# Two fused attention layers on one core: the first two key tiles of a unit are multiplied by halves of the tokens, x's high part before its low part, and the query product takes high parts before low parts

## The chip, the cores and the metric

One NeuronCore of a Trainium2 chip runs the whole program. The metric is the device time of one execution in microseconds (us); lower is better. Engines are called as in the profile: PE multiplies matrices, PEld is its load of the stationary operand, DVE, ACT and POOL are the vector, scalar and GpSimd engines, and SP issues most of the DMAs.

## The reference, cut to what matters

Two layers of the same form run one after the other over x, 8 batches of 512 tokens by 512 features, in float32. With `heads` = 8 in layer 0 and 16 in layer 1:

```python
xn  = layernorm(x) * ln_w + ln_b
q   = softmax_over_features_of_a_head(xn @ Wq + bq)
k   = softmax_over_tokens(masked(xn @ Wk + bk))
v   = masked(xn @ Wv + bv)
att = einsum("bnhd,bnhl->bhdl", k, v)          # layer 1: the same, other letters
y   = einsum("bnhd,bhdl->bnhl", q, att)
h   = silu(layernorm(y) * (1 + scale) + shift)  # scale, shift: a small product of emb
x   = x + h @ W_out + b_out
```

## The kernel before, in words

A **unit** is one batch of one layer; there are 16 (`UNITS`), u = 0 to 15, in the order of the batches, layer 0 first. Every float32 operand of a large product is split into a float16 high part and a float16 low part, and a product is the sum of three: high by high, high by low, low by high (`split_pairs`, and `product` at line 534, where nearly all matmuls are recorded).

PE does the units one after the other. In unit u (`step`) it makes, in this order:
- **K**: `project_keys(u)`, four tiles of 128 key features by 512 tokens. A tile is 4 chunks of the features by 3 products, 12 matmuls of 512 columns, with the weights as the stationary operand and x transposed (`xt_hi`, `xt_lo`, in the tile `xt_parts`) as the moving one. In the rows these read `ring<-sb_xt_parts,sb_w_hi` and `...,sb_w_lo`.
- **V** and **Q**: `project_tokens`, again 48 matmuls each, with x as the stationary operand (`ring<-sb_w_hi,sb_xt_parts`).
- **A**: `attention(u)`, 96 small matmuls (line 658; in unit 0 line 690).
- **O**: `output(u - 1)`, 48 matmuls of the unit before, from `ht_hi` and `ht_lo` (tile `ht_parts`).
- **Y**: `attend(u)`, 96 matmuls of 64 columns (line 709): the queries transposed (`qt_hi`, `qt_lo`, which lie in the tile `k_or_qt`) by the attention matrix.

The last unit (`last_unit`) has Q before V and splits O; unit 0 (`first_unit`) starts with `first_keys`, which is not changed.

The other engines follow: DVE takes each tile of the ring out of PSUM (`masked_keys`, `values`, `queries`, `residual`), does the statistics of Y (`attended_all`: `attended` line 1130, `y_statistics`, `centre` line 1147, which frees a bank pair of Y) and a part of each softmax. Its order in a unit is written out: `keys_beside_h`, `values`, `queries`, `mask_attention`, `query_sums`, the four `residual`s (line 1120, x_new), then `attended_all`. ACT has the exponents, the tanh and the high parts, POOL the low parts.

**The transposes** are DMAs from SBUF to SBUF, issued by SP in an order written out by hand in its `step(u)`: keys (`turn_k`), h (`turn_h`), the first two token tiles of the next unit's x (`turn_x(u, 0)`), queries (`turn_q`), the last two token tiles of x (`turn_x(u, 1)`), each the high part and then the low part:

```python
turn_k(u)
turn_h(u)
...
load_rows(u)
if u < LAST:
    turn_x(u, 0)
turn_q(u)
if u < LAST:
    turn_x(u, 1)
```

A completed transpose raises `xt_hi_ready` or `xt_lo_ready` by 16, so both stand at 32 * u when all of the x of unit u is turned and at 32 * u - 16 when its first half is. `step` and `last_unit` of the kernel before wait for both at 32 * u ahead of K, and `attend` for `qt_hi_ready` and `qt_lo_ready` ahead of its first matmul.

**PSUM**: the ring has six banks. `previous_users` works out from the order of all tiles who must have left a bank, and `take_bank` waits for it. K tiles 0 to 3 use banks 0 to 3. Banks 0 and 1 were O tiles 2 and 3 of the unit before (freed by `residual`), banks 2 and 3 hold the first pair of Y (freed by `centre`).

Of the kernel before, what the change touches and what calls it, by code (L numbers as in the profile page):

```python
# [5 lines left out]
P = 128  # L6
LAYERS = 2
B, S, D, E = 8, 512, 512, 1024
T = S // P
C = D // P  # L10
# [39 lines left out]
def layer_of(u):  # L50
    return u // B
# [55 lines left out]
def build(nc, x_d, emb_d, mask0_d, mask1_d, w_d, bias_d, wemb_d, cols_d, ident_d, blocks_d, out_d):  # L107
    with ExitStack() as ctx:
# [105 lines left out]
        def tile(buffer, a, b):  # L214
            return buffer[:, (4 * a + b) * P:(4 * a + b + 1) * P]
# [29 lines left out]
        def att_count(u):  # L245

            return C + u + (C - 1 if u == LAST else 0)
# [271 lines left out]
        def _(pe):  # L519
# [44 lines left out]
            def project_keys(u, tiles=range(C), between=lambda i: None):  # L564
                hi, lo = w_hi[layer_of(u)][K_], w_lo[layer_of(u)][K_]
                for i in tiles:
# [3 lines left out]
                                             lambda c: xt_hi[:, :, c, :], lambda c: xt_lo[:, :, c, :])).then_inc(done["K"], 1)  # L570
                    between(i)

            def project_tokens(name, unit, m, a_hi, a_lo, tiles=range(T), between=lambda i: None):
                hi, lo = w_hi[layer_of(unit)][m], w_lo[layer_of(unit)][m]
                for i in tiles:
                    out = take_bank(name, i, unit)
                    product(out, split_pairs(lambda c: a_hi[:, i, c, :], lambda c: a_lo[:, i, c, :],
                                             lambda c: hi[:, c, :], lambda c: lo[:, c, :])).then_inc(done[name], 1)
                    between(i)
# [110 lines left out]
                                last = nc.tensor.matmul(att_ps[:, c, :], lhs, rhs, start=(c == t == n == 0), stop=(c == C - 1 and t == T - 1 and n == 2))  # L690
                last.then_inc(att_summed, 1)

            def attend(u, between=lambda t: None):
                pe.wait_ge(qt_hi_ready, 16 * (u + 1))
                pe.wait_ge(qt_lo_ready, 16 * (u + 1))
                if u not in Q_FIRST:
                    pe.wait_ge(att_lo_ready, att_count(u))
                for t in range(T):
                    if t % 2 == 0:
                        take_bank("Y", t, u)  # L700
                    for c in range(C):
                        if u in Q_FIRST and t == 0:
                            pe.wait_ge(att_lo_ready, (att_count(u - 1) if u else 0) + c + 1)
                        hi, lo = tile(qt_hi, t, c), tile(qt_lo, t, c)
                        pairs = ((hi, att_hi), (hi, att_lo), (lo, att_hi))
                        for n, (lhs, rhs) in enumerate(pairs):
                            for j in range(2):
                                g = slice(j * HALF, j * HALF + HALF)
                                last = nc.tensor.matmul(y_at(t)[:, j, c * HALF:c * HALF + HALF], lhs[g, :], rhs[g, c, g], start=(n == 0), stop=(n == 2))  # L709
                    last.then_inc(done["Y"], 1)  # L710
                    between(t)

            def first_unit():
                def with_k(i):
# [32 lines left out]
            def step(u):  # L747
                shifted = PREPARED[1][u - PREP] if PREP <= u < PREP + 3 else None

                def with_k(i):  # L750
                    if u == 3 and i == 3:
                        turn_table(1)

                def with_q(i):
                    if u == 2 and i < 2:
                        film_product(1, i)
                    if shifted is not None and i == 0:
                        pe.wait_ge(h_ready, 4 * u)
                        shift_parts(1, shifted)
                    elif shifted is not None and i == 2:  # L760
                        shift_sums(1, shifted)

                def with_o(i):
                    if u == 2 and i == 0:
                        turn_film(1)
                    elif u == 2 and i == 3:
                        bound_film(1)
                    if PREP <= u < PREP + 4 and i == 3:
                        sum_w(1, PREPARED[1][u - PREP])

                pe.wait_ge(xt_hi_ready, 32 * u)
                pe.wait_ge(xt_lo_ready, 32 * u)
                if u == B:
                    pe.wait_ge(w_ready[1], 1)
                project_keys(u, between=with_k)
                if u == B:
                    pe.wait_ge(w_ready[1], 2)
                project_tokens("V", u, V_, xt_hi, xt_lo)
                if u == B:
                    pe.wait_ge(w_ready[1], 3)  # L780
                project_tokens("Q", u, Q_, xt_hi, xt_lo, between=with_q)
                if shifted is not None:
                    pe.wait_ge(shift_folded, folded(1, shifted))
                pe.wait_ge(h_ready, 4 * u)
                attention(u)
                if u == 1:
                    pe.wait_ge(o0_ready, 1)
                if u == B + 1:
                    pe.wait_ge(w_ready[1], 4)
                pe.wait_ge(ht_hi_ready, 16 * u)  # L790
                pe.wait_ge(ht_lo_ready, 16 * u)
                output(u - 1, between=with_o)
                attend(u)

            def last_unit(u):
                pe.wait_ge(xt_hi_ready, 32 * u)
                pe.wait_ge(xt_lo_ready, 32 * u)
                project_keys(u)
                project_tokens("Q", u, Q_, xt_hi, xt_lo)
                project_tokens("V", u, V_, xt_hi, xt_lo)  # L800
                pe.wait_ge(ht_hi_ready, 16 * u)
# [1050 lines left out]
```

## Time and profile before

| | us |
|---|---|
| median of 3 executions | 802.58 (800.82 to 805.05) |
| span of the profiled execution, first to last instruction | 799.5 |
| PE busy | 761.5 (95%) |
| DVE busy | 697.7 (87%) |
| ACT busy | 517.5 (65%) |
| POOL busy | 438.5 (55%) |
| DMA engines, share of 16 engines' time in the queue of SP | 70.8% |

The profiled execution's own time is its span and the start and end around it; it is one of the kind of the three above, and 802.58 - 799.5 = 3.1 us is what lies around the span at the median. The profile is read by the idle time that stands in front of a group or an instruction and by what released it. A completed DMA transpose is not shown as a releaser: a wait for it reads "issue". A matmul's end is modelled, so PE seems busy for a further 0.2 to 0.4 us after its last start; start to start is the sure reading.

### The profile page before, as it was taken

Reading aid. Unit: us, or ns where it says so; the run is one execution under the profiler, and the core shown is the slowest. Engines: PE = TensorE matmul, PEld = TensorE weight load, DVE = VectorE, ACT = ScalarE, POOL = GpSimd, SP = SyncE. Lnnn points to the kernel's source line nnn. Section 1 sums busy time; section 2 is a strip of 40 time slices with the busy share of each in tenths; the row PEclk is TensorE's granted clock in tenths of the full one; section 3 lists DMA queues with packets and bytes.
Section 4 is the critical chain, followed back from the end, with each engine's and each line's share of the span. In section 5 each row is a group of like instructions: output and inputs, shape, how many; then the busy total and the mean of one; then the engine's idle time right before and its main releaser. Section 6 shows DMA issues by size and latency. Waiting matters only on the chain.

```text
span 799.5 us, 16864 instructions
## 1 busy us (share of the span) xinstructions
PE 761.5 (95%) x6359; PEld 370.6 (46%) x6359; DVE 697.7 (87%) x1427; ACT 517.5 (65%) x1011; POOL 438.5 (55%) x433
## 2 busy tenths in 40 slices
PE   5997999999999999998999999999999999999986
PEld 2445444454544445444444544444454544444442
DVE  7898978798998999999988898898888889888885
ACT  5896766666667686885856685665767575560633
POOL 2465573663737767486672755447364545546323
PEclk9997999999999999999999999999999999999999
DMA  9976895856939769595794939487684939477462
GB/s 327 297 142 183 253 184 176 158 139 162 182 128 158 198 137 201 134 200 148 137 220 87 204 93 180 151 159 198 99 198 113 190 123 185 112 139 153 80 132 80
DMA packets 291249, 130.73 MB, mean 164 GB/s; under 512 B 261440, under 2 KB 261824, under 8 KB 291168
## 3 DMA queue, kind: packets, MB, share of 16 engines
q1 hardware_dynamic: 288432, 125.27, 70.8%
q10 hardware_dynamic: 2736, 4.39, 1.5%
q8 instruction: 50, 0.82, 0.4%
q14 instruction: 31, 0.25, 0.1%
HBM read 47.74 MB, written 16.88 MB: 81 GB/s over the span
## 4 chain that ended last, share of the span: by engine, by line
PE 85%; DVE 9%; issue 3%; ACT 2%; DMA 0%; POOL 0%; SPq 0%; DVEq 0%; ACTq 0%; POOLq 0%
PE ring L534 75%; PE ring L709 3%; PE att_ps L658 3%; DVE sb_k_or_qt L1042 1%; DVE sb_row_peak L881 1%; ACT sb_k_or_qt L1440 1%; DVE sb_q_sum L1101 1%; PE ring L834 0%; PE att_ps L595 0%; PE film_ps L595 0%; DVE sb_q_max L1075 0%; DVE ring L1072 0%; DVE sb_ht_parts L1158 0%; PE film_ps L604 0%; DMA sb_x<-in_x 0%
## 5 line engine op out<-in xcount | busy, mean ns | idle before, releaser
L534 PE MATMUL ring<-sb_w_hi,sb_xt_parts 128*128 128x512 f16 x1024 | 309.0, 379 | 0.0
L534 PE MATMUL ring<-sb_w_lo,sb_xt_parts 128*128 128x512 f16 x512 | 194.0, 379 | 0.0
L534 PE MATMUL ring<-sb_w_hi,sb_ht_parts 128*128 128x512 f16 x512 | 155.8, 379 | 4.0 <-ACT sb_ht_parts L1610 1.4
L534 PEld LDWEIGHTS ring<-sb_w_hi,sb_xt_parts 128*128 128x128 f16 x1024 | 100.4, 98 | 126.0 <-issue 6.6
L534 PE MATMUL ring<-sb_xt_parts,sb_w_hi 128*128 128x512 f16 x496 | 148.6, 381 | 9.7 <-issue 9.1
L1698 POOL TENSOR_TENSOR sb_htok<-sb_ht_parts,sb_htok 128x512 f16<-128x512 f32 x60 | 75.0, 1272 | 137.8 <-ACT sb_htok L1473 137.8
L1714 POOL TENSOR_TENSOR sb_tanh<-sb_v_or_q,sb_kq_hi 128x512 f16<-128x512 f32 x64 | 74.1, 1159 | 87.7 <-ACT sb_kq_hi L1504 87.1
L534 PE MATMUL ring<-sb_w_lo,sb_ht_parts 128*128 128x512 f16 x256 | 97.0, 379 | 0.0
L534 PE MATMUL ring<-sb_xt_parts,sb_w_lo 128*128 128x512 f16 x248 | 94.5, 381 | 0.0
L1497 ACT ACTIVATE sb_v_or_q<-ring,sb_ln_one 128x512 f32<-128x512 f32 x64 | 43.9, 686 | 61.0 <-DVE ring L1077 60.9
L1689 POOL TENSOR_TENSOR sb_x<-sb_x,sb_bias_o 128x512 f32<-128x512 f32 x64 | 79.3, 1274 | 5.9 <-DVE sb_w_lo L958 5.9
L534 PEld LDWEIGHTS ring<-sb_w_hi,sb_ht_parts 128*128 128x128 f16 x512 | 50.1, 98 | 63.4 <-ACT sb_ht_parts L1610 4.1
L534 PEld LDWEIGHTS ring<-sb_xt_parts,sb_w_hi 128*128 128x128 f16 x496 | 47.5, 98 | 67.2 <-issue 12.3
L534 PEld LDWEIGHTS ring<-sb_w_lo,sb_xt_parts 128*128 128x128 f16 x512 | 50.1, 98 | 59.4 <-issue 0.7
L1709 POOL TENSOR_TENSOR sb_tok<-sb_v_or_q,sb_tok 128x512 f16<-128x512 f32 x56 | 66.4, 1199 | 17.1 <-ACT sb_tok L1436 17.1
L1417 ACT ACTIVATE sb_v_parts<-sb_x,sb_x_minus 128x512 f16<-128x512 f32 x52 | 36.9, 710 | 58.4 <-POOL sb_x_minus L1670 58.4
L1120 DVE SCALAR_TENSOR_TENSOR sb_x<-ring,sb_down_o,sb_x 128x512 f32<-128x512 f32 x60 | 43.2, 748 | 28.3 <-PE ring L534 26.0
L1042 DVE SCALAR_TENSOR_TENSOR sb_k_or_qt<-sb_k_or_qt,sb_k_recip,sb_kq_hi 128x512 f16<-128x512 f32 x64 | 61.5, 961 | 5.1
L1440 ACT ACTIVATE sb_k_or_qt<-sb_k_or_qt,sb_k_shift 128x512 f32<-128x512 f32 x64 | 45.4, 710 | 20.3 <-DVE sb_k_shift L1029 20.3
L1432 ACT ACTIVATE sb_v_or_q<-sb_x,sb_x_add,sb_x_rstd 128x512 f32<-128x512 f32 x56 | 43.9, 808 | 22.2 <-POOL sb_x_add L1677 22.2
L1464 ACT ACTIVATE att_ps<-sb_ht_parts,sb_scale_down 128x512 f32<-128x512 f32 x30 | 20.6, 687 | 57.6 <-DVE sb_ht_parts L1153 57.5
L1072 DVE SCALAR_TENSOR_TENSOR ring<-ring,sb_scale_down,sb_bias_q 128x512 f32<-128x512 f32 x64 | 48.0, 750 | 9.1 <-PE ring L534 9.0
(232 smaller groups left out, 1401.0 us busy)
## 6 DMA issues: line engine op xcount, KB each, us to landing
out<-sb_x SPq DMA_DIRECT2D x14, 1024.0 KB, 4.9
sb_rows_now<-film_rows SPq DMA_DIRECT2D x16, 512.0 KB, 4.5
sb_x<-out SPq DMA_DIRECT2D x8, 1024.0 KB, 5.2
sb_x<-in_x SPq DMA_DIRECT2D x7, 1024.0 KB, 5.4
sb_mask_add<-mask_terms SPq DMA_DIRECT2D x15, 256.0 KB, 5.5
sb_w_hi<-in_L_cond_W_emb SPq DMA_DIRECT2D x1, 1536.0 KB, 14.1
sb_w_lo<-in_L_cond_W_emb SPq DMA_DIRECT2D x1, 1536.0 KB, 14.4
sb_w_hi<-in_L_cond_film_emb_W ACTq DMA_DIRECT2D x1, 1536.0 KB, 11.9
```

The lines of the kernel that those rows point to most:

```text
L534: last = nc.tensor.matmul(out, lhs, rhs, start=(n == 0), stop=(n == len(pairs) - 1))
L1042: nc.vector.scalar_tensor_tensor(out=k_lo[:, i * S:i * S + S], in0=k_or_qt[:, i, :], scalar=k_recip[:, i:i + 1], in1=kq_hi[:, i * S:i * S ...
L1072: nc.vector.scalar_tensor_tensor(out=here, in0=here, scalar=scale_down[:, layer, Q_:Q_ + 1], in1=bias_q[layer][:], op0=ALU.mult, op1=ALU.a ...
L1120: nc.vector.scalar_tensor_tensor(out=xt(unit, t), in0=bank("O", t, unit), scalar=down_o[:, layer:layer + 1], in1=xt(unit, t), op0=ALU.mult ...
L1417: nc.scalar.activation(unused(unit)[:, t, :], xt(unit, t), ACT.Square, bias=x_minus[:, t:t + 1], accum_out=x_square[:, t:t + 1]).then_inc( ...
L1432: nc.scalar.activation(xh_of(unit)[:, t, :], xt(unit, t), ACT.Identity, bias=x_add[:, t:t + 1], scale=x_rstd[:, t:t + 1]).then_inc(xh_read ...
L1440: nc.scalar.activation(k_or_qt[:, i, :], k_or_qt[:, i, :], ACT.Exp, bias=k_shift[:, i:i + 1], accum_out=k_sum[:, i:i + 1]).then_inc(k_exp, 1)
L1497: nc.scalar.activation(q[:, t, :], bank("Q", t, u), ACT.Exp, bias=ln_one[:]).then_inc(q_exp, 1)
L1689: nc.gpsimd.tensor_tensor(xt(u, t), xt(u, t), bias_o[layer][:], ALU.add).then_inc(x_biased, 1)
L1698: nc.gpsimd.tensor_tensor(hp_lo[:, t, :], y_of(unit)[:, t, :], hp_hi[:, t, :], ALU.subtract).then_inc(h_lo_ready, 1)
L1709: nc.gpsimd.tensor_tensor(xp_lo[:, t, :], xh_of(unit)[:, t, :], xp_hi[:, t, :], ALU.subtract).then_inc(xp_lo_ready, 1)
L1714: nc.gpsimd.tensor_tensor(q_lo[:, t * D:t * D + D], q[:, t, :], kq_hi[:, t * D:t * D + D], ALU.subtract).then_inc(q_lo_ready, 1)
```

## The change

A new `keys_by_halves(u)` makes key tiles 0 and 1 of the units 1 to 15. It takes both banks at the start, then waits only for the first half of the tokens (both parts) and makes all three products of both tiles for tokens 0 to 255; then it waits for the second half of x's high part and makes the two products that use it; then for the second half of the low part and makes the last one. That is 24 + 16 + 8 = 48 matmuls of 256 columns in place of 24 of 512. Tile 0 and tile 1 are both finished in the last eight. Tiles 2 and 3 follow by `project_keys(u, (2, 3))` as before. `attend` takes its token tiles in two pairs: for a pair the products with the high queries come first (32 matmuls), then, for the first pair, the wait for `qt_lo_ready`, then those with the low queries (16 matmuls). The number of its matmuls is the same. SP, DVE, ACT and POOL have the same instructions in the same order.

```diff
+            def keys_by_halves(u):
+
+                hi, lo = w_hi[layer_of(u)][K_], w_lo[layer_of(u)][K_]
+                outs = [take_bank("K", i, u).rearrange("p (t m) -> p t m", t=T) for i in range(2)]
+                pe.wait_ge(xt_hi_ready, 32 * u - 16)
+                pe.wait_ge(xt_lo_ready, 32 * u - 16)
+                for i in range(2):
+                    f = slice(i * P, i * P + P)
+                    for c in range(C):
+                        for n, (w, xs) in enumerate(((hi, xt_hi), (hi, xt_lo), (lo, xt_hi))):
+                            nc.tensor.matmul(outs[i][:, 0:2, :], w[:, c, f], xs[:, 0:2, c, :], start=(c == n == 0), stop=False)
+                pe.wait_ge(xt_hi_ready, 32 * u)
+                for i in range(2):
+                    f = slice(i * P, i * P + P)
+                    for c in range(C):
+                        for w in (hi, lo):
+                            nc.tensor.matmul(outs[i][:, 2:4, :], w[:, c, f], xt_hi[:, 2:4, c, :], start=False, stop=False)
+                pe.wait_ge(xt_lo_ready, 32 * u)
+                for i in range(2):
+                    f = slice(i * P, i * P + P)
+                    for c in range(C):
+                        last = nc.tensor.matmul(outs[i][:, 2:4, :], hi[:, c, f], xt_lo[:, 2:4, c, :], start=False, stop=(c == C - 1))
+                    last.then_inc(done["K"], 1)
+
...
-            def attend(u, between=lambda t: None):
+            def attend(u):
                 pe.wait_ge(qt_hi_ready, 16 * (u + 1))
-                pe.wait_ge(qt_lo_ready, 16 * (u + 1))
                 if u not in Q_FIRST:
                     pe.wait_ge(att_lo_ready, att_count(u))
-                for t in range(T):
-                    if t % 2 == 0:
-                        take_bank("Y", t, u)
-                    for c in range(C):
-                        if u in Q_FIRST and t == 0:
-                            pe.wait_ge(att_lo_ready, (att_count(u - 1) if u else 0) + c + 1)
-                        hi, lo = tile(qt_hi, t, c), tile(qt_lo, t, c)
-                        pairs = ((hi, att_hi), (hi, att_lo), (lo, att_hi))
-                        for n, (lhs, rhs) in enumerate(pairs):
+                for pair in ((0, 1), (2, 3)):
+                    take_bank("Y", pair[0], u)
+                    for t in pair:
+                        for c in range(C):
+                            if u in Q_FIRST and t == 0:
+                                pe.wait_ge(att_lo_ready, (att_count(u - 1) if u else 0) + c + 1)
+                            for n, part in enumerate((att_hi, att_lo)):
+                                for j in range(2):
+                                    g = slice(j * HALF, j * HALF + HALF)
+                                    nc.tensor.matmul(y_at(t)[:, j, c * HALF:c * HALF + HALF], tile(qt_hi, t, c)[g, :], part[g, c, g],
+                                                     start=(t % 2 == c == n == 0), stop=False)
+                    if pair[0] == 0:
+                        pe.wait_ge(qt_lo_ready, 16 * (u + 1))
+                    for t in pair:
+                        for c in range(C):
                             for j in range(2):
                                 g = slice(j * HALF, j * HALF + HALF)
-                                last = nc.tensor.matmul(y_at(t)[:, j, c * HALF:c * HALF + HALF], lhs[g, :], rhs[g, c, g], start=(n == 0), stop=(n == 2))
-                    last.then_inc(done["Y"], 1)
-                    between(t)
+                                last = nc.tensor.matmul(y_at(t)[:, j, c * HALF:c * HALF + HALF], tile(qt_lo, t, c)[g, :], att_hi[g, c, g],
+                                                        start=False, stop=(t == pair[1] and c == C - 1))
+                        last.then_inc(done["Y"], 1)
...
-                pe.wait_ge(xt_hi_ready, 32 * u)
-                pe.wait_ge(xt_lo_ready, 32 * u)
                 if u == B:
                     pe.wait_ge(w_ready[1], 1)
-                project_keys(u, between=with_k)
+                keys_by_halves(u)
+                project_keys(u, (2, 3), between=with_k)
...
             def last_unit(u):
-                pe.wait_ge(xt_hi_ready, 32 * u)
-                pe.wait_ge(xt_lo_ready, 32 * u)
-                project_keys(u)
+                keys_by_halves(u)
+                project_keys(u, (2, 3))
```

## Rows read from the trace of the kernel before

**Rows 1.** The page: busy time and share of each engine, and the granted clock.
```profile
PE 761.5 (95%) x6359; PEld 370.6 (46%) x6359; DVE 697.7 (87%) x1427; ACT 517.5 (65%) x1011; POOL 438.5 (55%) x433
PEclk9997999999999999999999999999999999999999
```

**Rows 2.** Chain that ended last, 540 to 640 us: start, us, what.
```profile
548.42 0.31 issue
548.73 31.24 PE ring L534 x144
...
592.07 1.51 PE ring L709 x96
593.58 0.49 issue
```

**Rows 3.** Groups of the page: busy, mean ns of one, idle before them, releaser.
```profile
L534 PE MATMUL ring<-sb_xt_parts,sb_w_hi 128*128 128x512 f16 x496 | 148.6, 381 | 9.7 <-issue 9.1
```

**Rows 4.** Timeline of PE where K starts: start us, us, what, idle before it.
```profile
122.36 0.59 PE L534 MATMUL ring<-sb_xt_parts,sb_w_hi 128*128 128x512 f16 x2 [1.48 <-issue]
...
365.12 0.59 PE L534 MATMUL ring<-sb_xt_parts,sb_w_hi 128*128 128x512 f16 x2 [2.19 <-issue]
411.36 0.59 PE L534 MATMUL ring<-sb_xt_parts,sb_w_hi 128*128 128x512 f16 x2 [0.85 <-issue]
...
503.56 0.59 PE L534 MATMUL ring<-sb_xt_parts,sb_w_hi 128*128 128x512 f16 x2 [1.01 <-issue]
...
594.07 0.59 PE L534 MATMUL ring<-sb_xt_parts,sb_w_hi 128*128 128x512 f16 x2 [0.49 <-issue]
594.50 0.38 PE L534 MATMUL ring<-sb_xt_parts,sb_w_lo 128*128 128x512 f16 x1
...
730.98 0.59 PE L534 MATMUL ring<-sb_xt_parts,sb_w_hi 128*128 128x512 f16 x2 [1.20 <-issue]
```

**Rows 5.** Timeline of SP's queue, transposes of queries and x, late in unit 11.
```profile
586.55 2.54 SPq L410 DMA_TRANSPOSE sb_k_or_qt<-sb_tanh  x1
589.21 2.89 SPq L410 DMA_TRANSPOSE sb_xt_parts<-sb_tok  x2
```

**Rows 6.** DMA issues: count, median us to landing.
```profile
sb_xt_parts<-sb_tok SPq DMA_TRANSPOSE x60, 3.8
```

**Rows 7.** Timeline of PE: the seam from Y to K where nothing is waited for.
```profile
221.39 0.20 PE L709 MATMUL ring<-sb_att_hi,sb_k_or_qt 64*128 64x64 f16 x2
221.51 0.61 PE L534 MATMUL ring<-sb_xt_parts,sb_w_hi 128*128 128x512 f16 x2
```

**Rows 8.** Timeline of PE where Y or O starts late, four places.
```profile
350.78 0.38 PE L534 MATMUL ring<-sb_w_hi,sb_ht_parts 128*128 128x512 f16 x1 [0.52 <-issue]
408.93 0.20 PE L709 MATMUL ring<-sb_att_hi,sb_k_or_qt 64*128 64x64 f16 x2 [0.47 <-issue]
500.97 0.21 PE L709 MATMUL ring<-sb_att_hi,sb_k_or_qt 64*128 64x64 f16 x2 [0.60 <-issue]
771.49 0.21 PE L709 MATMUL ring<-sb_att_hi,sb_k_or_qt 64*128 64x64 f16 x2 [1.67 <-issue]
```

**Rows 9.** Timeline of PE, 128-column matmuls of unit 0, from 62.80 us.
```profile
62.80 1.17 PE L690 MATMUL att_ps<-sb_v_parts,sb_kt_or_y 128*128 128x128 f16 x18
```

**Rows 10.** Timeline of PEld at the start of K in unit 12.
```profile
594.04 0.13 PEld L534 LDWEIGHTS ring<-sb_xt_parts,sb_w_hi 128*128 128x128 f16 x2 [0.59 <-issue]
```

**Rows 11.** Timeline of DVE around the starts of K in units 7 and 8.
```profile
361.41 0.75 DVE L1120 SCALAR_TENSOR_TENSOR sb_x<-ring,sb_down_o,sb_x 128x512 f32<-128x512 f32 x1 [0.32 <-PE ring L534]
...
365.41 1.30 DVE L1130 TENSOR_TENSOR ring<-ring,sb_q_recip 128x512 f32<-128x512 f32 x2
...
368.30 1.40 DVE L1147 SCALAR_TENSOR_TENSOR sb_ht_parts<-ring,sb_y_mean_var,sb_rows_now 128x512 f32<-128x512 f32 x2
...
408.57 0.75 DVE L1120 SCALAR_TENSOR_TENSOR sb_x<-ring,sb_down_o,sb_x 128x512 f32<-128x512 f32 x1 [1.84 <-PE ring L534]
409.85 1.30 DVE L1130 TENSOR_TENSOR ring<-ring,sb_q_recip 128x512 f32<-128x512 f32 x2 [0.53 <-PE ring L709]
...
418.75 0.74 DVE L1021 CUSTOM_DVE_ANT_0 sb_k_or_qt<-ring,sb_mask_add,sb_scale_down 128x512 f32<-128x512 f32 x1
```

## The prediction

> **What bounds the kernel now.** I read the page first. PE is busy 95% of the span and runs at full clock but for one slice; DVE follows with 87% [rows 1]. Then the chain of waits, in order of time. One unit is 45.2 us there (548.42 to 593.58), and all of it is PE but a piece called "issue" between Y and K: 0.31 us ahead of unit 11, 0.49 ahead of unit 12 [rows 2]. So there is little to win except these pieces. The groups add them up: the first matmuls of K have 9.7 us of idle time ahead of them, 9.1 of it "issue" [rows 3]. The timeline shows them one by one, nine of over 0.2 us, the longest 1.48 in unit 2 and 2.19 in unit 7 [rows 4].
>
> What is waited for is a transpose, which the profile does not name as a releaser. In unit 11, SP issues the low queries' transpose at 586.55 and the two of x's second half at 589.21 to 592.10; the low one goes out near 590.7, and with the median of 3.8 us to landing it arrives at about 594.5 [rows 5, 6]. K starts at 594.07 [rows 4]. The first half of x was turned ahead of the queries. So the wait is for the last quarter of x, the low part of the second half, and the high part is there some 1.4 us sooner.
>
> **The change part by part.**
>
> *The waits ahead of K.* The stalls sum to 9.1 us [rows 3]. Idle time is counted from a modelled end 0.2 us after the last start of Y, and with no wait K starts 0.12 us after that start [rows 7], so each of the nine is 0.08 longer: 9.1 + 9 * 0.08 = 9.8 us. In the new order the last quarter is needed only after 40 matmuls of 256 columns, 40 * 0.109 = 4.4 us after K starts (pace below), the high one after 24, 2.6 us. The longest stall is 2.27 us, so each is covered with 2 us in hand. Removed: **9.8 us**.
>
> *The matmuls.* 24 of 512 columns become 48 of 256. Two of 512 start 0.43 us apart, 215 ns each [rows 4]; 18 of 128 columns with a full 128 by 128 load each take 1.17 - 0.22 = 0.95 us from first to last start, 56 ns each [rows 9]. A line through the two is 0.415 ns a column and 2.8 ns a matmul, so one of 256 takes 109 ns. Price: 24 * 2.8 = 0.07 us a unit, 15 units: **1.0 us**. Bounds: nothing (if half the columns took half the time), and 24 * 8.5 = 0.2 us a unit, 3 us in all, if each 256 columns ran at the pace of two 128s. The line lies between them, and I take it. The loads are 24 more too. That a load hides behind 128 columns is in rows 9: the pace there, 56 ns, is the columns' own. The Trainium skill (TensorE: Matmul & The Clock Gate, section "Back-to-back issue gap") speaks against that: a stream of loads and matmuls of 128 columns takes about 81 ns each. By it a matmul of 256 columns would take an estimated 134 ns and the change would cost 18 us, not 1. The trace does not agree, with 56 ns where the page says 81.
>
> *Tile 0 done later.* It was done 2.6 us after K's start and is now done after 44 matmuls, 4.8 us. DVE waits for it, but DVE is on the statistics of Y until 418.75, when it turns to key tile 0, 7.4 us after that K's start [rows 11]. Cost nothing; if DVE were over 2.6 us faster there it would be up to 2.2 us a unit.
>
> *Bank 1 taken early.* Tile 1's bank is now wanted at K's start, not 2.6 us later. It is freed by the last residual, which ends at 408.57 + 0.75 = 409.3, while Y is still running and 2 us ahead of that K [rows 11]. Nothing.
>
> *Y with the high queries first.* 32 matmuls before the wait for the low ones. 96 take 1.39 us (592.07 to 593.58, less the seam of 0.12) [rows 2, 7], so 32 are 0.46 us of cover. Three late starts of Y are 0.47, 0.60 and 1.67 us [rows 8]. Each gives up to 0.46, together **1.4**; the lower end is 1.0, if the low queries come later against PE than now. The first pair is finished no later than before, so DVE loses nothing.
>
> *What is late next.* DVE's order from Y to the next queries has hardly a wait for PE in it, and behind it hang ACT's and POOL's parts and the transposes of h and queries. That path starts at the end of O (residual) or the first pair of Y and takes about as long as PE's round, and it does not get shorter when K starts sooner. Three places:
> - Unit 7, with the 2.27 us stall. DVE was late there: it finished the last residual at 362.2, then did scales until 365.41, and the two centres that free banks 2 and 3 end at 368.30 + 1.40 = 369.7 [rows 11]. K would now start at 362.85, want bank 2 at + 5.2 = 368.1, and wait 1.6 us for it. Add 0.3 at O, whose h comes down the same path: 1.9 of the 2.27 given back.
> - O in units 6, 8 and 10. In unit 6 O already waited 0.52 us for h [rows 8] with almost no stall ahead of K. In units 8 and 10 the stalls ahead of K were 0.93 and 1.09 (idle and 0.08) [rows 4]; I take half as given back, 1.0, and 0.1 for unit 6. Ends: none and all 2.0.
> - Unit 15, where Y waits 1.67 us for its queries [rows 8], which do not come from PE's progress alone: 0.5 of its 1.28 us [rows 4] back.
>
> In all **3.5 us** given back; the ends are 1 us (no h wait, a centre that comes sooner) and 7 (every later unit bound by DVE's path).
>
> **Sum:** 9.8 + 1.4 - 1.0 - 3.5 = 6.7 us off the profiled span of 799.5: 792.8, and with the 3.1 us around it **795.9 us** against the median of 802.58 (0.8% less).
>
> **The rivals.**
> 1. *The other engines' path sets the round* (DVE's order, then ACT, POOL and the transposes of h and queries). For it: DVE is 87% busy [rows 1], Y and O each have waits for transposes [rows 8], and PE is at most 1 us a unit behind that path. Against it: DVE stands idle for 1.84 us each unit waiting for O's last tile [rows 11], so the path restarts with PE, not by itself. If it held in units 7 to 15, the gain left would be that of unit 2 (1.5), Y's 1.4 and about 0.8 from the rest, less 1.0 for the matmuls: 802.6 - 2.7 = 799.9 us.
> 2. *Slower: the loads are no longer hidden.* Place: the 48 matmuls of each `keys_by_halves`. Where nothing covers a load the matmul starts 31 ns after it, 594.04 to 594.07 [rows 4, 10]. If each of the 720 new matmuls lost that, 22 us: 795.9 + 22.3 = 818 us. It decides against the change from 6.7 us / 720 = 9 ns a matmul. Against it: 56 ns for 128 columns [rows 9]. The page named above gives 25 ns of such a loss, an estimated 814 us.
> 3. *The stall is not the transpose.* If "issue" were PE's own start of a new shape, it would stay, and the change would cost its 1.0 us: 803.6. Against it: a seam with no stall at all [rows 7] and lengths from 0.31 to 2.19 [rows 2, 4].
> 4. *Nothing is given back.* 9.8 + 1.4 - 1.0 = 10.2 us off: 792.4.
>
> **How the numbers follow.** A change under 0.5% (4.0 us) is what a measurement of this kernel can hardly tell from none; three runs spread over 4.2 us. Forecast (3 to 9 us off, faster by over 0.5% in most of it): 0.74. Rival 1: 0.16. Rival 2: 0.04. Rival 3: 0.03. Rival 4: 0.03. Faster by over 0.5% (below 798.6): nearly all of the forecast and rival 4, 0.76. Within: rivals 1 and 3 and the weak end of the forecast, 0.20. Slower: 0.04. The range runs from just below rival 4's end, 792.0, to 799.6, just short of rival 1, and so leaves out some 2 in 10.
>
> **What would show it.** Right: "issue" ahead of K's matmuls goes from 9.1 us to under 1; the 256-column matmuls start 109 ns apart; in unit 7 PE waits 1 to 2 us in the middle of K for DVE line 1147; a new or longer wait stands ahead of O in units 8 and 10; Y starts with less idle time. Wrong: starts 120 ns apart or more; DVE newly waiting for key tile 0; waits ahead of O and inside Y that sum to 6 us or more; or K's stall still there in its last eight split matmuls.

## The result, and the profile after

The changed kernel takes **791.65 us** (median of 4 runs, 790.94 to 793.91) against 802.03 us for the kernel before, run beside it: ratio 0.9881 [0.9864, 0.9898], faster by 1.2%. On the median the prediction was made against, 802.58, that ratio gives 793.0 us, inside the predicted 792.0 to 799.6. The raw median lies 0.35 us under the low end. The profiled execution spans 789.9 us (own time 791.66), 9.6 us less than before. The sum had said 6.7.

The page of the changed kernel, answering to [rows 1] and to the group of [rows 3], and below it, from the list of groups, the group that K now starts with:

```profile
PE 761.1 (96%) x6719; PEld 405.4 (51%) x6719; DVE 696.8 (88%) x1427; ACT 517.4 (65%) x1011; POOL 439.4 (56%) x433
...
PEclk9998999999999999999999999999999999999999
...
L534 PE MATMUL ring<-sb_xt_parts,sb_w_hi 128*128 128x512 f16 x256 | 76.2, 379 | 1.8 <-DVE sb_ht_parts L1174 1.8
...
L583 PE MATMUL ring<-sb_xt_parts,sb_w_hi 128*128 128x256 f16 x240 | 41.5, 278 | 0.0
```

PE does 360 matmuls more in the same busy time (761.1 us, 761.5 before), so what went is idle time. The 9.1 us of "issue" in that group is gone, the 256-column group at K's start has no idle time ahead of it, and 1.8 us of a wait for DVE are new.

The changed kernel's chain of waits, 540 to 600 us (start, us, what), against [rows 2]:

```profile
541.93 0.47 PE ring L730 x32
542.39 0.23 PE ring L738 x16
542.63 2.73 PE ring L583 x24
545.36 1.75 PE ring L589 x16
547.10 0.87 PE ring L594 x8
547.98 25.90 PE ring L534 x120
...
587.48 2.73 PE ring L583 x24
```

The unit is now 44.85 us (542.63 to 587.48), and no "issue" stands between Y (lines 730, 738) and K (583, 589, 594). Before it was 45.2.

The changed kernel's PE, waits by the line that waited (us in total, times, longest), without those that stand in the first and last units:

```profile
PE ring L534 <- DVE sb_ht_parts L1174: 1.8, 2, 1.5
...
PE ring L534 <- issue: 1.2, 3, 0.6
...
PE ring L738 <- DMA sb_k_or_qt<-sb_tanh: 0.7, 2, 0.4
```

Three lines answer to three steps of the prediction: a wait in the middle of K, what is left of "issue" (ahead of O in units 6 and 7 and in the last unit, none ahead of K), and the low queries, now waited for separately.

The changed kernel's timeline of PE, the four places that matter (start us, us, what, idle before it):

```profile
367.99 0.60 PE L534 MATMUL ring<-sb_xt_parts,sb_w_hi 128*128 128x512 f16 x2 [1.49 <-DVE sb_ht_parts L1174]
...
587.42 0.39 PE L583 MATMUL ring<-sb_xt_parts,sb_w_hi 128*128 128x256 f16 x2
587.65 0.27 PE L583 MATMUL ring<-sb_xt_parts,sb_w_lo 128*128 128x256 f16 x1
587.75 0.38 PE L583 MATMUL ring<-sb_xt_parts,sb_w_hi 128*128 128x256 f16 x2
...
721.39 0.41 PE L738 MATMUL ring<-sb_att_hi,sb_k_or_qt 64*128 64x64 f16 x16 [0.27 <-DMA sb_k_or_qt<-sb_tanh]
...
762.33 0.41 PE L738 MATMUL ring<-sb_att_hi,sb_k_or_qt 64*128 64x64 f16 x16 [0.43 <-DMA sb_k_or_qt<-sb_tanh]
```

Three matmuls of 256 columns take 587.75 - 587.42 = 0.33 us from start to start, 0.11 each. The wait at 367.99, in K of unit 7, is for DVE's centre, as foretold.

**Where the 9.6 us came from**, start to start, units 1 to 15 summed, after minus before:

```
last Y start -> first K start    -10.07   (before: 10.1 over 0.12 each; after: 0)
K, first to last start            +2.51   (unit 7: +1.74; the other fourteen: +0.77)
K's end -> O's start              +0.30   (unit 7: 0.29; units 6, 8, 10: 0.05, 0.00, 0.04)
O                                 -0.05
O's end -> last Y start           -2.11   (unit 7 -0.54, 9 -0.67, 15 -1.13, 10 +0.08, 14 +0.15)
ahead of unit 1's K               -0.20
```

### The profile page after: what moved, and what is told of

Same layout as the page of the kernel before. It is cut to its first block, busy times and chain, and to the rows that moved or that the text cites. A ratio compares the mean times of both kernels' runs of the same rounds, so it can differ in the third digit from the quotient of the medians.

```text
span 789.9 us, 17598 instructions
## 1 busy us (share of the span) xinstructions
PE 761.1 (96%) x6719; PEld 405.4 (51%) x6719; DVE 696.8 (88%) x1427; ACT 517.4 (65%) x1011; POOL 439.4 (56%) x433
## 4 chain that ended last, share of the span: by engine, by line
PE 80%; DVE 12%; ACT 3%; issue 2%; DMA 2%; SPq 1%; POOL 0%; DVEq 0%; ACTq 0%; POOLq 0%
PE ring L534 62%; PE ring L583 5%; PE ring L589 3%; PE att_ps L682 3%; PE ring L730 2%; PE ring L594 1%; DVE sb_k_or_qt L1069 1%; DMA sb_k_or_qt<-sb_tanh 1%; ACT sb_k_or_qt L1467 1%; PE ring L738 1%; DVE sb_row_peak L908 1%; DVE sb_q_max L1102 1%; DVE ring L1099 1%; DVE ring L1104 1%; DVE sb_q_sum L1128 1%
## 5 line engine op out<-in xcount | busy, mean ns | idle before, releaser
L534 PE MATMUL ring<-sb_xt_parts,sb_w_hi 128*128 128x512 f16 x256 | 76.2, 379 | 1.8 <-DVE sb_ht_parts L1174 1.8
L534 PE MATMUL ring<-sb_xt_parts,sb_w_lo 128*128 128x512 f16 x128 | 48.5, 379 | 0.0
L1180 DVE SCALAR_TENSOR_TENSOR sb_ht_parts<-sb_ht_parts,sb_y_rstd,sb_rows_now 128x512 f32<-128x512 f32 x60 | 47.1, 805 | 0.0
```

The lines of the kernel that those rows point to most:

```text
L534: last = nc.tensor.matmul(out, lhs, rhs, start=(n == 0), stop=(n == len(pairs) - 1))
L1180: nc.vector.scalar_tensor_tensor(out=y_of(unit)[:, t, :], in0=y_of(unit)[:, t, :], scalar=y_rstd[:, t:t + 1], in1=rows_now[:, 1, :], op0=A ...
```

## The experiments

Each kernel was timed in three rounds beside the kernel before on its chip; a ratio is to that. The "changed kernel" is the one of the diff.

### Each half alone

**The keys' part alone**: the changed kernel with the old `attend`.

```
-            def attend(u):                          # the changed one
+            def attend(u, between=lambda t: None):  # the one before
```

> The key tiles by halves alone, the query product as before. Theory A (the stall ahead of K was the wait for x's last quarter, and the other engines' path is not the bound): 'issue' ahead of K under 1 us, the gain 8 to 9.5 us of the whole change's 10; Y keeps late starts of up to 0.5 us in the units where its low queries land last. Theory B (the other engines' path sets the round, and the gain needs the later wait in Y as well): under 6 us, with more idle time ahead of Y than before.

Measured: 794.28 us, ratio 0.9912 [0.9893, 0.9931], 7.1 us off. At the median this is less than theory A's band and more than theory B's (the interval gives 5.5 to 8.6 us), so neither can be said to have had it right. All K stalls are gone (-10.07), K is 2.94 longer, and Y starts late. Its PE timeline and wait list:

```profile
497.43 0.20 PE L733 MATMUL ring<-sb_att_hi,sb_k_or_qt 64*128 64x64 f16 x2 [0.87 <-issue]
...
764.62 0.20 PE L733 MATMUL ring<-sb_att_hi,sb_k_or_qt 64*128 64x64 f16 x2 [1.94 <-issue]
```

```profile
PE ring L733 <- issue: 3.5, 4, 1.9
```

The 0.87 and 1.94 us ahead of the first matmul of Y were 0.60 and 1.67 before [rows 8]: with K early, the queries come a little later against PE. So Y's order seems to be worth more on top of the first part than the 1.4 of the prediction: 794.28 less 791.65 or, in the later run below, 792.46 is 2.6 or 1.8 us. The intervals of the ratios overlap slightly, so the times alone don't prove it; stage by stage the two profiles differ by 2.8 us from O's end to Y's.

**Y's part alone**: the kernel before with the new `attend`.

```
-            def attend(u, between=lambda t: None):  # the one before
+            def attend(u):                          # the changed one
```

> The query product's new order alone, K as before. Theory A: Y's late starts shrink, but K still waits for x's last quarter, which lands a fixed time behind the queries, so what Y gains is waited for ahead of K: the time is the same within 1.5 us, and the idle time ahead of K grows. Theory B: 1.4 us or more faster, since the first pair of Y restarts DVE sooner.

Measured: 800.24 us, 0.9988 [0.9977, 1.0], no difference beyond the measurement. Theory A had the time right but not the way there: in the profile Y gave 1.27, and K's stalls did not grow but shrank by 1.64. But K of unit 7 is 1.7 us longer, because the clock fell. In the windows view of this kernel (columns: window, its length, busy time of PE, PEld, DVE, ACT and POOL, granted clock, DMA share, GB/s):

```profile
361.50:364.90 3.40, 1.66 (x99) 1.52 (x97) 2.98 (x10) 0.00 (x0) 3.40 (x4) 1.00 1.19 185
364.90:368.50 3.60, 3.44 (x9) 1.23 (x10) 3.38 (x10) 2.71 (x7) 0.85 (x2) 0.53 0.51 196
368.50:371.90 3.40, 3.40 (x17) 1.54 (x16) 3.37 (x9) 1.69 (x5) 2.08 (x4) 1.00 0.72 264
```

After a stall of 1.97 us the granted clock averages 0.53 over the next 3.6 us (the level of 1.2 GHz nearly throughout) where the kernel before, after a stall of 2.27, kept 1.00. The columns took the time and PE was "busy" meanwhile, so no list of waits shows this loss.

### Is it the transpose, and are the loads hidden?

**The split with none of its use**: both waits for x stand at K's start, 256 columns, old `attend`.

```
             def keys_by_halves(u):
...
-                pe.wait_ge(xt_hi_ready, 32 * u - 16)
-                pe.wait_ge(xt_lo_ready, 32 * u - 16)
+                pe.wait_ge(xt_hi_ready, 32 * u)
+                pe.wait_ge(xt_lo_ready, 32 * u)
```

(and the two later waits are gone)

> The 256-column matmuls alone: both key tiles are made by halves, but all four waits for x stand at the start, and the query product is as before. My price of 2.8 ns a matmul: 1.0 us slower than before, starts 109 ns apart. Rival (loads no longer hidden, 31 ns each): 22 us slower. Half-size matmuls at no price: the same.

Measured: 803.82 us, 1.0027 [1.0016, 1.0038], 2.2 us slower (1.3 to 3.0), more than my 1.0. Rival 2's 22 us are excluded: K goes from 10.14 to 10.20 us, 0.06 a unit, 0.8 us in all. In the profile the largest other piece is again the clock, in unit 10. The other executions agree: their mean granted clock is 0.992 (ten), against 0.995 for the kernel before (twenty). The PE timeline and the wait list of this kernel:

```profile
502.62 0.58 PE L583 MATMUL ring<-sb_xt_parts,sb_w_hi 128*128 128x256 f16 x2 [2.45 <-DMA sb_xt_parts<-sb_tok]
503.01 0.42 PE L583 MATMUL ring<-sb_xt_parts,sb_w_lo 128*128 128x256 f16 x1
503.22 0.63 PE L583 MATMUL ring<-sb_xt_parts,sb_w_hi 128*128 128x256 f16 x2
...
503.86 0.63 PE L583 MATMUL ring<-sb_xt_parts,sb_w_hi 128*128 128x256 f16 x2
```

```profile
PE ring L583 <- DMA sb_xt_parts<-sb_tok: 9.9, 9, 2.5
```

Three matmuls take 0.64 us there (503.22 to 503.86), twice as long as at full clock, and that K is 11.78 us long, 1.6 more. And the stall that was called "issue" is now named: a wait for x's transpose, 9 times, 9.9 us. A DMA that is waited for can appear under either name.

**SP's order**: the kernel before, with x's second half turned ahead of the queries.

```
+                if u < LAST:
+                    turn_x(u, 1)
                 turn_q(u)
                 if u < LAST:
-                    turn_x(u, 1)
                     sp.wait_ge(x_new, 4 * u)
```

> The kernel before with one change in SP's order: the transposes of x's second half are issued ahead of the queries' ones instead of behind them; PE's program is untouched. Theory A: SP is idle between the last Q tile on PE and the last high query, about 4 us, and the two issues take 2.9, so the queries' transposes are hardly later, x is there when Y ends, and the stalls ahead of K vanish without 256-column matmuls: 8 to 11 us faster. Theory C (the transposes share the DMA engines, and an earlier one for x makes the one for the queries late): the idle time moves from K to Y, and the gain is under 4 us.

Measured: 805.64 us, 1.0059 [1.0039, 1.0079], slower. The queue in unit 11 (timeline of SP), and the wait list of PE:

```profile
579.95 7.33 SPq L410 DMA_TRANSPOSE sb_xt_parts<-sb_tok  x4
587.47 1.36 SPq L410 DMA_TRANSPOSE sb_k_or_qt<-sb_kq_hi  x1
588.95 3.49 SPq L410 DMA_TRANSPOSE sb_k_or_qt<-sb_tanh  x1
```

```profile
PE ring L710 <- issue: 15.0, 12, 2.3
```

Theory C had it: the idle time moved from K to Y, for a loss. K's stalls are all gone (-10.07), which shows that they are the transposes of x's second half, last in SP's queue, and rival 3 falls. But the low queries' transpose is issued later: at 588.95, 38.5 us after the start of its unit's K, where it was 37.8 us [rows 2, 5]. Y starts late, by 0.65 us more in this unit and by 12.7 us more in sum. One transfer is last in this queue; the change under study makes that one harmless instead of moving it.

### Is the split needed?

**High part first, 512 columns**: the changed kernel, where K's first two tiles are taken whole, 16 high matmuls, then the wait, then 8 low ones (the loops shortened to words).

```
-                pe.wait_ge(xt_hi_ready, 32 * u - 16)
...
+                pe.wait_ge(xt_hi_ready, 32 * u)
+                for i in range(2): ...   w_hi, w_lo x xt_hi[:, :, c, :]
+                pe.wait_ge(xt_lo_ready, 32 * u)
+                for i in range(2): ...   w_hi x xt_lo[:, :, c, :]
```

> The changed kernel with keys_by_halves replaced: both tiles keep 512 columns, K waits at its start for all of x's high part, makes 16 matmuls with it, and only then waits for the low part (3.5 us later). Query product as in the changed kernel. If only the last quarter of x was late, and the split into 256 columns is paid for: 1 us faster than the changed kernel (about 12 less than the kernel before), less what K now waits for the high part, which landed 0.1 to 0.7 us ahead of K's start in most units. If the first half's early start matters too: 1 to 3 us slower than the changed kernel.

Measured: 793.38 us, 0.9918 [0.9903, 0.9933]. Three short stalls come back ahead of K (0.26, 0.30 and 0.34 us, units 2, 8 and 10), and its profile has a fall of the clock in the last unit, worth 1.5 us. So most of the gain, 6.6 us of some 9, needs no halves at all, only the high part ahead of the low one. But I had expected it to be 1 us faster than the changed kernel, and it is 2 to 3 us slower: its interval lies just above the 0.9881 [0.9864, 0.9898] of the result and overlaps the later 0.989 [0.9873, 0.9908]. That is the size foretold for the case that the first half's early start matters; the profile, with 0.9 us of stalls ahead of K, shows a part of it only.

**One tile by halves**: tile 0 split, tile 1 whole and high part first (the edit in words).

```
-                for i in range(2):     # both tiles [:, 0:2, :], then [:, 2:4, :]
+                tile 0: xt[:, 0:2], wait high, xt_hi[:, 2:4]; tile 1: xt_hi whole;
+                wait low; tile 0: xt_lo[:, 2:4]; tile 1: xt_lo whole
```

> The changed kernel with only key tile 0 by halves; tile 1 keeps 512 columns, high part first: 12 matmuls of 256 columns need the first half alone (1.3 us), then come 8 of 256 and 8 of 512 with the high part (2.6 us), so the last quarter of x is wanted 3.9 us after K's start. It landed 1.1 to 2.7 us after it in the changed kernel and the high part at most 0.3 us after it, so nothing stalls, and K is 24 * 1.4 ns = 0.03 us shorter: 0.5 us faster than the changed kernel, or the same as far as three rounds tell. If the high part is wanted too early: PE waits at line 587 or so in several units, slower than the changed one.

Measured: 795.21 us, 0.9921 [0.9899, 0.9943]. No stall ahead of K, and the extra matmuls cost about half, as expected. But it is not 0.5 us faster: at the median it is 2.8 us slower than the changed kernel run beside it (792.46; the intervals overlap). Half a us of that lies outside the span (2.3 us around it, 1.8 in the others), and in its profile the low queries were later in units 9 and 15. Its timeline of PE:

```profile
498.09 0.41 PE L739 MATMUL ring<-sb_att_hi,sb_k_or_qt 64*128 64x64 f16 x16 [1.38 <-DMA sb_k_or_qt<-sb_tanh]
...
764.43 0.41 PE L739 MATMUL ring<-sb_att_hi,sb_k_or_qt 64*128 64x64 f16 x16 [1.08 <-DMA sb_k_or_qt<-sb_tanh]
```

In unit 9 the low transpose landed 4.2 us after the high one, not the usual 2.3. Whether this comes from the edit or from the run stays open.

### The 1.5 us in unit 7

**The scales later**: the changed kernel; in unit 6, whose scales DVE does from 360.3 to 363.6 in the changed kernel's timeline, they are moved behind `attended_all`.

```
-                if prepares is not None:
+                if prepares is not None and prepares != O_:
                     find_scale(1, prepares)
-                if prepares == O_:
-                    output_scale(1)
-                    v_scales(1)
                 attended_all(u)
+                if prepares == O_:
+                    find_scale(1, prepares)
+                    output_scale(1)
+                    v_scales(1)
```

> The changed kernel; in unit 6 DVE's scale work for the last weight of layer 1 (13 small instructions, 3.2 us) stands behind the statistics of Y instead of ahead of them. My step: the 1.49 us that PE waits in K of unit 7 for line 1174 is that delay, so it goes, and the whole kernel is 1.5 us faster than the changed one (some 12 less than before). Rival: the wait only moves (to O of unit 7, whose h comes down the same path): under 0.7 us.

Measured: 792.19 us, 0.9902 [0.9887, 0.9917]; against the changed kernel nothing can be told. The wait inside K of unit 7 is gone, which shows it to be DVE's scales ahead of the centre. A new one stands at the same unit's A (this kernel's timeline of PE):

```profile
394.20 1.71 PE L682 MATMUL att_ps<-sb_v_parts,sb_kt_or_y 128*64 128x64 f16 x96 [0.91 <-POOL sb_v_parts L1731]
```

The wait is for POOL's low values, so it seems that these hang on the scales too. K of unit 7 is 1.67 us shorter than in the changed kernel, A starts 0.93 us later behind it and O another 0.07, and 0.66 us is left at unit 8's start. So the rival had it ("under 0.7 us"): most of the wait only moved.

### How long is the path behind DVE?

The prediction took the path that begins with DVE's first step on Y and ends with the landed low queries to be "about as long as PE's round". Dead DVE time in every unit was to measure its slack.

**1.48 us ahead of `attended_all`**, in the kernel before and in the changed one:

```
             def attended_all(u):
+                for n in range(3):
+                    link(nc.vector.memset(pad[:], 0.0))   # 128 x 384
```

> The kernel before with three linked memsets of 384 columns (about 1 us together) on DVE ahead of the statistics of Y in every unit: work that nothing needs, in the path from Y to the next queries. If that path was as long as PE's round, as I held, each us of it costs nearly a us in the units 7 to 15: 6 to 12 us slower. If it had slack, under 3 us.

> The changed kernel with the same useless work on DVE. Theory A (the later waits for x and for the low queries have given the path slack): less is lost than in the kernel before, by 2 to 6 us. Theory B (the path bounds the changed kernel, which has no stalls left to hide it in): more is lost than in the kernel before, 10 us or more.

Measured: 814.01 us, 1.0172 [1.0155, 1.0189], and 805.31 us, 1.0065 [1.0049, 1.0082]. By the changed kernel's ratio it would be 0.9881 * 800.15 = 790.6 on this chip, so the pads cost 13.9 and 14.7 us, the same. Theory A's "less is lost" for the changed kernel is wrong, and theory B's "more" is not shown by the times. The 13.9 is also above the 6 to 12 I had expected. The wait lists of PE, before with pads and changed with pads:

```profile
PE ring L535 <- issue: 13.1, 12, 1.7
PE ring L535 <- DVE sb_ht_parts L1148: 5.7, 4, 2.0
```

```profile
PE ring L535 <- DVE sb_ht_parts L1175: 7.1, 5, 2.9
...
PE ring L535 <- issue: 3.3, 4, 1.6
```

Where the loss fell tells more than the sum. Between K's starts in units 8 and 15 stand seven pads, 10.4 us. Over that stretch they cost 2.5 us in the kernel before (319.6 to 322.2) and 5.3 us in the changed one (314.5 to 319.9), so here, in one profile of each, theory B's "more is lost" holds. Another 8.7 and 8.5 us were lost ahead of unit 8, mostly in the middle of K in units 4 to 7, where PE waits for DVE's centre (L1148 and L1175 above) and where in both kernels the clock fell once (last section).

The path has no length that could be read from the pitch of the units, because it is not a round of its own. In both padded kernels DVE still stands and waits for PE's last tile of O, 1.0 to 2.2 us in each of the units 8 to 14. From their timelines of DVE, unit 11, before with pads and changed with pads:

```profile
602.20 0.75 DVE L1121 SCALAR_TENSOR_TENSOR sb_x<-ring,sb_down_o,sb_x 128x512 f32<-128x512 f32 x1 [1.84 <-PE ring L535]
```

```profile
596.93 0.75 DVE L1148 SCALAR_TENSOR_TENSOR sb_x<-ring,sb_down_o,sb_x 128x512 f32<-128x512 f32 x1 [1.66 <-PE ring L535]
```

So the path starts anew from PE in every unit, and 1.48 us more on it need not make the unit 1.48 us longer. What room it has is read from the landings in the changed kernel. In units 8, 9, 11, 12 and 13 the low queries landed 0.4 to 1.5 us before PE came to the products with them, in unit 10 at the same moment, in units 14 and 15 0.4 and 0.5 us after. h's low part landed 0.4 to 2.2 us ahead of O in units 8 to 15, but for unit 10, where O had just to wait for it. "About as long as PE's round" was near, with room in most units and none in some.

**0.95 us between key tiles 2 and 3**:

```
                 masked_keys(u, 2)
+                link(nc.vector.memset(pad[:], 0.0))
+                link(nc.vector.memset(pad[:], 0.0))
                 masked_keys(u, 3)
```

> The kernel before with two linked memsets (0.95 us) on DVE between key tile 2 and key tile 3 of the units 1 to 15. Theory D (in the kernel before the path from Y to the next queries does depend on PE: DVE stands waiting for key tile 3 by 0.3 to 1.2 us in the units 2, 8, 9, 13 and 15, because the stall ahead of K made it late): there the added work is partly free, and the time from DVE's first step on Y to the landing of the low queries grows by 0.1 to 0.7 us in these units and by 0.95 in the others. Theory E (the path owes nothing to PE, as the prediction had it): it grows by 0.95 in all.

> The changed kernel with the same two memsets. Theory D: DVE no longer waits for key tile 3 there, so the same path grows by 0.95 us in every unit from 8 on, and the kernel loses more in the units 8 to 15 than the kernel before does. Theory E: the same growth and the same loss in both.

Measured: 811.6 us, 1.0127 [1.0104, 1.0149], and 802.11 us, 1.0015 [1.0004, 1.0025]; the losses are 10.6 and 9.7 us (the latter against the changed kernel run beside it). I had put these pads where the kernel before waits for PE, to see them swallowed there. From DVE's timeline of the kernel before, units 8, 9 and 13:

```profile
422.01 0.06 DVE L864 MEMSET sb_spare<- 128x1 f32 x1 [0.26 <-PE ring L534]
...
467.69 0.06 DVE L864 MEMSET sb_spare<- 128x1 f32 x1 [0.91 <-PE ring L534]
...
650.33 0.06 DVE L864 MEMSET sb_spare<- 128x1 f32 x1 [0.85 <-PE ring L534]
```

Those waits did shrink, from 3.97 us over the run (with 1.24 in unit 2 and 0.71 in unit 15) to 1.02. From the start of key tile 2 to that of key tile 3 the units 8 to 15 took 5.8 us more in the kernel before and 8.0 in the changed one, so some 2 us were swallowed. The whole path of these units grew by 7.4 us in the kernel before (351.7 to 359.1) and by 9.4 in the changed one (347.4 to 356.8). Unit by unit theory D did not come true: in the kernel before the path grew by 0.7 to 1.6 us in units 8, 9, 13 and 15, where it should have grown least, and by 0.5 to 0.9 in the others. And the loss from unit 8 to unit 15 was 4.1 and 4.3 us, alike, where the theory had the changed kernel lose more. These two runs show that the waits exist and can take up part of a delay. They don't show how much of the gain is due to them.

**The changed kernel again**, beside these two:

```
(no edit)
```

> The changed kernel itself, for a comparison on the same chip: 10 us faster than before; a PE stall of over 1.5 us is only that in K of unit 7, and the clock stays full from 80 us to the end.

Measured: 792.46 us, 0.989 [0.9873, 0.9908], 8.6 us off, span 790.7. The 1.5 us of unit 7 is a 1.72 here, and the clock is full from 78 us on.

## Why the prediction was right, and where not

**The waits ahead of K** (9.8 us): 10.07 measured, every one gone. The cover sufficed everywhere: the last quarter of x landed at most 2.65 us after K's start (unit 14; 2.5 in unit 10, 2.2 in unit 7) against the 4.4 in hand. That it is the transpose was shown by SP's order and by the split without early start.

**The matmuls** (1.0 us, 0.07 a unit): 0.8 us in fourteen units, starts 109 ns apart in the whole of `keys_by_halves`. The loads stay hidden. The Trainium skill (TensorE: Matmul & The Clock Gate, section "Back-to-back issue gap") gives about 81 ns a matmul for a stream of loads and matmuls of 128 columns, and the 134 ns and 814 us were estimates worked out from that. The trace agrees with neither: it has 56 ns at 128 columns [rows 9] and 109 at 256.

**Tile 0 and bank 1** (nothing): DVE waits for key tile 0 nowhere in units 7 to 15, and no K of these units starts late. Right.

**Unit 7** (1.9 given back): 1.67 in K (1.74 less 0.07) and 0.29 at O. The mechanism (DVE's scales, then the centre that frees the bank) was shown for the wait in K by moving the scales.

**Y** (1.4): 2.3 us in units 7, 9 and 15, less 0.2 elsewhere. Units 7 and 9 gave 0.54 and 0.67, the whole of their waits, for which 0.46 of cover had been counted. Unit 15 gave 1.13, since its queries' path was shorter as well (42.3 us before, 40.4 after). What the order costs where queries are late shows in unit 14: the high ones are in time, and the wait of 0.27 falls in the middle of Y.

**The step that failed** is the one that said of the path behind DVE that it "takes about as long as PE's round, and it does not get shorter when K starts sooner", and with it that DVE's order has "hardly a wait for PE in it". From it came 1.1 us given back at O in units 6, 8 and 10, and 0.5 in unit 15. Measured: 0.05, 0.00 and 0.04 at O, and in unit 15 a gain. The prediction had half of the contrary in hand: against rival 1 it set that DVE idles 1.84 us in each unit waiting for O's last tile. Two things stand in the step's place. The path had room: in the kernel before h's low part landed 0.41 and 0.45 us ahead of O in units 8 and 10, where half of the stall was charged. And it did get shorter, from DVE's first step on Y to the landed low queries over units 8 to 15 from 351.7 to 347.5 us. The timeline of the kernel before has a part of the reason, in the stretch from [rows 11] on that I took for free of waits: DVE waits for PE's key tile 3, 0.26, 0.91, 0.85 and 0.71 us in units 8, 9, 13 and 15. In the changed kernel, where K starts sooner, none of them is left. In its timeline of DVE the same step of unit 8 starts with no idle ahead of it:

```profile
417.96 0.74 DVE L1048 CUSTOM_DVE_ANT_0 sb_k_or_qt<-ring,sb_mask_add,sb_scale_down 128x512 f32<-128x512 f32 x1
...
418.66 0.06 DVE L891 MEMSET sb_spare<- 128x1 f32 x1
```

They are 2.7 of the 4.2 us; with the waits too short for the lists, the step from key tile 2 to key tile 3 is 3.1 us shorter in all. Most of the rest, 0.9 us, lies in DVE's statistics of Y, where the same instructions took less time; why stays open. h's own path, from the same first step to the landing of h's low part, went from 33.9 to 31.3 us in unit 8, where 1.7 of it is that the low transpose landed 4.0 us behind the high one before and 2.3 after, and from 34.0 to 33.4 in unit 10. That the shorter path comes from K's earlier start is shown for the waits alone.

So of the 2.9 us between the sum (6.7) and the span (9.6), 1.5 were given back on paper only (1.6 less the 0.1 measured), and 0.7 are Y's larger gain (2.11 for 1.4). The other 0.7 are K's (0.3 in stalls, 0.2 in columns) and the start (0.2). Rival 1 fell with the same step. Rival 4 (nothing given back, 10.2 us off) came nearer than the sum, though it was given a chance of 0.03: it left out the 2.0 us of unit 7 and, the other way, Y's larger gain and the 0.7 of K and the start. The 3.1 us around the span was a misreading: in the executions of both kernels listed here it is 1.8, and the 3.1 came from taking the median and the span of different executions. So the raw median is lower still.

## What to carry to other kernels

When a transfer is last in its queue and its reader stalls, look first whether the reader can begin with what has landed; reordering the queue only chooses another who waits, here for a loss. Before a saving is called "given back later", walk the other path for its own waits on the engine that will now be sooner: each is slack, and the path has no fixed length. Splitting a matmul into halves was nearly free here (3 ns each), and taking the high part first with whole columns brought 6.6 us of some 9 without it.

## What the hardware showed that I had not expected

A stall of PE can cost more than its length. After stalls of 1.97 us (Y's part alone) and 2.52 us (the split with none of its use), the granted clock was at the lower level for some 3.4 us, and the K behind it took 1.6 to 1.7 us more. It doesn't always happen: the kernel before had 2.27 us at 365.12 with the clock at 1.00 all along. The high-first kernel's last unit shows one more, in its windows view:

```profile
770.00:773.00 3.00, 1.66 (x10) 0.84 (x8) 2.81 (x5) 1.57 (x3) 0.00 (x0) 1.00 0.00 0
773.00:777.00 4.00, 3.73 (x10) 1.44 (x11) 3.73 (x10) 1.49 (x3) 0.54 (x1) 0.57 0.00 0
```

PE had been busy 1.66 of 3 us before it fell. Each kernel with the 1.48 us pads has such a fall too, in the middle of K: the kernel before from 279 us, in unit 5, and the changed kernel from 376 us, in unit 7, after 5 us in which PE was busy for 2.06. The latter's windows view:

```profile
371.00:376.00 5.00, 2.06 (x15) 1.23 (x14) 4.92 (x12) 3.42 (x6) 3.33 (x6) 1.00 0.53 167
376.30:379.80 3.50, 3.50 (x10) 1.24 (x9) 3.42 (x10) 1.27 (x3) 2.52 (x3) 0.51 0.27 105
```

The changed kernel, with no stall of more than 1.8 us behind its first unit, had none of these falls in either profile after the first 78 us. Nothing shows the change to be a protection against them: the kernel before had none in its profile either, and the mean granted clock of the executions is 0.995 for the changed kernel (eight) and 0.995, 0.995 and 0.997 for the kernel before (twenty, thirteen and seven, on three chips).

The other is that the landing of a transpose varies for the same instruction. The low queries are usually 2.3 to 2.4 us behind the high ones, and 4 us in single units: 14 in the changed kernel (717.36 and 721.34), 9 in the kernel with one tile split; and so was h's low part in unit 8 of the kernel before. It is not mere chance. In unit 14 the gap is 3.95 to 4.05 us in all five profiles of the changed kernel, alone or with its scales moved or its DVE padded, and 2.4 with either half of the change alone and in the two kernels that make the first tiles otherwise. The 1.6 us more that it takes is larger than most terms of the sum. No run here says what decides it.
